# Triangular inverse in a cleared buffer of its own, basis norms taken from the inner products, and the rounding exponent by one integer operation

## The reference, cut to what matters

```python
G = Kc.T @ Kc + RIDGE_EPS * I            # 64 x 64
W = jnp.linalg.solve(G, Kc.T @ Vc)
U = I[:, :8]
for _ in range(2):
    U, _ = jnp.linalg.qr(W @ U)
S_new = 0.9 * S + U @ (U.T @ W)
out = 0.125 * (Qc @ S_new)
```

## Time and profile before

| | |
|---|---|
| runs, median (lowest to highest) | 1487.51 us (1479.54 to 1488.72) |
| profiled execution, its own time | 1489.35 us |
| its span, first to last instruction | 1487.5 us |
| TensorE matmul busy | 969.3 us (65%) |
| VectorE busy | 1230.2 us (83%) |
| ScalarE busy | 640.3 us (43%) |
| GpSimd busy | 231.3 us (16%) |
| TensorE's mean granted clock | 0.825 of full |

### The profile page before, as it was taken

How to read it: one execution, slowest core, us unless ns; L and a number is a source line. 1 busy time by engine, 2 the same in 40 slices (tenths; PEclk the granted TensorE clock), 3 DMA queues, 4 the chain that set the end, 5 groups by cost and what they waited for, 6 DMA issues and landing times.

```text
span 1487.5 us, 43627 instructions
## 1 busy us (share of the span) xinstructions
PE 969.3 (65%) x17726; PEld 780.0 (52%) x17726; DVE 1230.2 (83%) x3729; ACT 640.3 (43%) x1294; POOL 231.3 (16%) x149
## 2 busy tenths in 40 slices
PE   1443940389177799787799787852819825996175
PEld 0332530365167667677667686742717624775154
DVE  5885659949999779996799996798875798878997
ACT  3663630156135466555466454431416512563152
POOL 3552001101111001113102023012140000021000
PEclk9855985589579899899899898785959957898597
DMA  2555110001000001001101002030030200111000
GB/s 78 168 167 194 46 44 0 1 18 50 8 4 4 4 10 46 2 4 50 54 17 38 3 4 86 4 123 0 4 125 19 75 1 17 50 47 32 9 25 24
DMA packets 52086, 61.60 MB, mean 41 GB/s; under 512 B 4048, under 2 KB 32416, under 8 KB 51888
## 3 DMA queue, kind: packets, MB, share of 16 engines
q1 hardware_dynamic: 51888, 58.84, 12.6%
HBM read 38.31 MB, written 20.51 MB: 40 GB/s over the span
## 4 chain that ended last, share of the span: by engine, by line
DVE 36%; PE 32%; issue 13%; ACT 5%; POOL 2%; DMA 1%; SPq 0%; DVEq 0%; POOLq 0%; ACTq 0%
PE a_bank L840 5%; PE a_bank L830 3%; PE a_bank L846 3%; DVE a_total L1581 3%; DVE a_outer L1579 3%; DVE a_blocks L1584 3%; DVE a_outer L1575 2%; PE a_bank L946 2%; PE a_bank L961 2%; PE a_bank L769 2%; PE a_bank L898 2%; PE a_bank L698 2%; DVE a_blocks L1586 2%; DVE a_recip L1561 2%; PE a_bank L808 2%
## 5 line engine op out<-in xcount | busy, mean ns | idle before, releaser
L1092 ACT ACTIVATE a_work<-a_bank 128x512 f32<-128x512 f32 (+1 forms) x193 | 110.9, 599 | 206.5 <-PE a_bank L808 170.8
L1485 POOL TENSOR_TENSOR a_root<-a_recip,a_half 128x32 f32<-128x32 f32 (+2 forms) x24 | 89.8, 3743 | 655.8 <-DVEq L1570 636.9
L808 PE MATMUL a_bank<-a_ident,a_blocks 128*128 128x128 f32 x256 | 42.2, 340 | 162.6 <-DVE a_blocks L1595 162.6
L1092 ACT ACTIVATE a_solve<-a_bank 128x512 f32<-128x512 f32 (+2 forms) x184 | 87.9, 522 | 114.1 <-PE a_bank L846 53.9
L1575 DVE TENSOR_TENSOR a_outer<-a_blocks,a_weight 128x62 f32<-128x62 f32 (+15 forms) x248 | 129.4, 522 | 0.0
L1581 DVE TENSOR_REDUCE a_total<-a_outer 128x62 f32<-128x62 f32 (+30 forms) x248 | 127.0, 512 | 0.3
L808 PEld LDWEIGHTS a_bank<-a_ident,a_blocks 128*128 128x128 f32 x256 | 40.4, 208 | 163.7 <-DVE a_blocks L1595 163.7
L1579 DVE TENSOR_TENSOR a_outer<-a_blocks 128x60 f32<-128x60 f32 (+14 forms) x240 | 119.2, 497 | 0.7 <-DVE a_outer L1575 0.7
L1584 DVE TENSOR_TENSOR a_blocks<-a_blocks,a_outer 128x60 f32<-128x60 f32 (+14 forms) x240 | 118.3, 493 | 0.0
L698 PE MATMUL a_bank<-a_wk,a_cg 128*128 128x512 f32 x256 | 117.3, 602 | 0.0
L769 PE MATMUL a_bank<-a_scaled,a_blocks 128*128 128x352 f32 x256 | 90.6, 495 | 28.7 <-ACT a_scaled L1072 15.2
(11 more groups left out here) (200 smaller groups left out, 2402.4 us busy)
## 6 DMA issues: line engine op xcount, KB each, us to landing
f_x<-in_L_attn_x SPq DMA_DIRECT2D x16, 256.0 KB, 3.2
s_xnt<-f_xt SPq DMA_DIRECT2D x16, 256.0 KB, 2.1
s_c<-f_cm SPq DMA_DIRECT2D x16, 256.0 KB, 2.3
s_base<-f_base SPq DMA_DIRECT2D x16, 256.0 KB, 2.8
a_cg<-s_c SPq DMA_DIRECT2D x16, 256.0 KB, 2.9
a_cc<-s_c SPq DMA_DIRECT2D x16, 256.0 KB, 3.7
a_xnt<-s_xnt SPq DMA_DIRECT2D x16, 256.0 KB, 3.9
a_base_in<-s_base SPq DMA_DIRECT2D x13, 256.0 KB, 2.6
```

Of the source, the lines that this page charges most:

```text
L808: last = nc.tensor.transpose(bank[:, i * P:(i + 1) * P], rows_[:, :, 4 * rb + i], ident[:])
L1092: nc.scalar.activation(out, view, ACT.Copy, scale=scale).then_inc(emptied, 1)
L1485: nc.gpsimd.tensor_tensor(root[:, :, a:b], recip[:, :, a:b], half[:, :, a:b], ALU.pow).then_inc(roots_ok, 1)
```

## The change

`factor` gets a second buffer, `triangle`, of the same size. It is cleared and its diagonal set to one at the start of each call, before the wait for the call's input (which has moved into `factor`); `lead` and `schur` first wait for the end of the factor before, which used the buffer. The inverse grows in `triangle` (`x` in the code) and the factor stays in `block_` (`m`), so that the negated scaled columns stay there too. `weight` is gone: `known` multiplies by `m[:, :, 0:i, i]` in place. The update of the inverse covers one row more (`0:i` for `0:j`) and starts at step 0. The closing memsets are gone, and one multiplication over all 2 x 32 x 32 elements, from `x` to `m`, replaces two over parts.

`orthogonalise` multiplies a vector with itself and all later ones in one instruction; the first of the sums is the norm. The scaled copy is gone, and the sums are scaled instead. The two products L1626 are one instruction.

In `fp4_blocks` the exponent bits are ORed with a constant within L466; the clamp to 1.5 * 2**22 is the first half of two scalar_tensor_tensor instructions, which add it to, and subtract from it, the value. L467 is gone, and the sign that this turns is turned back in the last product.

The scratch for dynamic DMA descriptors is 4096 bytes where it was 8192.

```diff
--- before.py
+++ after.py
@@ -59,7 +59,7 @@
 T = GB_N * NC
 HB = 32
 KEPT = 16
-FACTOR_LINKS = 8 * (HB - 1) + 1
+FACTOR_LINKS = 7 * (HB - 1) + 4
 ROOTS = ((0, 16), (16, 28), (28, HB))
 LENGTHS = ((0, 6), (6, R))
 BANK = 512
@@ -444,7 +444,20 @@
...
+ROUNDER = 1.5 * 2.0 ** 22
+EXPONENT = 0x7F800000
+LARGE = (22 << 23) | (1 << 22)
...
 def fp4_blocks(nc, ch, jobs):
...
@@ -463,13 +476,12 @@
     each(lambda v, amax, scale, inv, step: V.tensor_scalar(scale, amax, 1.0 / 6.0, 1e-12, ALU.mult, ALU.max))
     each(lambda v, amax, scale, inv, step: V.reciprocal(inv, scale))
     each(lambda v, amax, scale, inv, step: V.tensor_tensor(v, v, bcast(inv, 2, QB), ALU.mult))
-    each(lambda v, amax, scale, inv, step: V.tensor_scalar(step.bitcast(I32), v.bitcast(I32), 0x7F800000, None, ALU.bitwise_and))
-    each(lambda v, amax, scale, inv, step: V.tensor_scalar(step, step, 1.0, 1.5 * 2.0 ** 22, ALU.max, ALU.mult))
-    each(lambda v, amax, scale, inv, step: V.tensor_tensor(v, v, step, ALU.add))
-    each(lambda v, amax, scale, inv, step: V.tensor_tensor(v, v, step, ALU.subtract))
+    each(lambda v, amax, scale, inv, step: V.tensor_scalar(step.bitcast(I32), v.bitcast(I32), EXPONENT, LARGE, ALU.bitwise_and, ALU.bitwise_or))
+    each(lambda v, amax, scale, inv, step: V.scalar_tensor_tensor(v, step, ROUNDER, v, ALU.max, ALU.add))
+    each(lambda v, amax, scale, inv, step: V.scalar_tensor_tensor(v, step, ROUNDER, v, ALU.max, ALU.subtract))
     for k, (v, amax, scale, inv, step, done) in enumerate(jobs):
         ch.wait(last[k])
-        V.tensor_tensor(v, v, bcast(scale, 2, QB), ALU.mult).then_inc(done, 1)
+        V.scalar_tensor_tensor(v, v, -1.0, bcast(scale, 2, QB), ALU.mult, ALU.mult).then_inc(done, 1)
...
 def fp4_weights(nc, ch, v, rows, nb, tmp):
@@ -572,7 +584,7 @@
         wkt, wvt, wqt = (blocks[:, i].rearrange("p (h m) -> p h m", m=P) for i in (1, 3, 5))
         recip, root, half = sb("recip", [P, 2, HB]), sb("root", [P, 2, HB]), sb("half", [P, 2, HB])
         outer_all = sb("outer", [P, 4 * KEPT * HB])
-        weight, total = sb("weight", [P, 2, HB]), sb("total", [P, 2, HB])
+        total, triangle = sb("total", [P, 2, HB]), sb("triangle", [P, 2, HB * HB])
         cg = [sb(f"cg{i}", [P, NC, D]) for i in range(2)]
         cc = sb("cc", [P, T, D])
         xa, xb, xc = (sb(n, [P, T, D]) for n in ("xa", "xb", "xc"))
@@ -1356,7 +1368,7 @@
         SUBSPACE_UNITS = 2 * (T // 4) + 2 * 2 + 2 * APPLY_UNITS + 4 + R // 4
         ASSEMBLE_UNITS = HB // 4 + 2 * (NQ // 32) + NQ // 8
 
-        LINKS = 2 * FACTOR_LINKS + 4 * R + 6 * (R - 1)
+        LINKS = 2 * FACTOR_LINKS + 4 * R + 3 * (R - 1)
 
         with nc.Block() as block:
 
@@ -1545,14 +1557,14 @@
                 dve.sem_inc(cg_used, 2)
                 dve.sem_inc(cc_used, 1)
 
-                def factor(block_, n, done):
...
-                    m = by_columns(block_)
-                    diagonal = block_[:, :, 0:HB * HB:HB + 1]
+                def factor(block_, n, given, done):
...
+                    m, x = by_columns(block_), by_columns(triangle[:])
+                    diagonal, ones = (y[:, :, 0:HB * HB:HB + 1] for y in (block_, triangle))
 
                     def area(at, a, b):
                         return outer_all[:, at:at + 2 * a * b].rearrange("p (s a b) -> p s a b", s=2, b=b)
@@ -1560,72 +1572,59 @@
                     def pivot(j):
                         return ch.inc(V.reciprocal(recip[:, :, j], m[:, :, j, j]))
 
+                    ch.link(V.memset(triangle[:], 0.0))
+                    ch.inc(V.memset(ones, 1.0))
+                    dve.wait_ge(*given)
                     ch.link(V.tensor_scalar(diagonal, diagonal, RIDGE_EPS, None, ALU.add))
                     inverse = pivot(0)
                     for j in range(HB - 1):
                         i, n_i = j + 1, HB - 1 - j
-                        row, rest = m[:, :, 0:j, j], m[:, :, 0:j, i:HB]
                         ch.wait(inverse)
                         if i in (ROOTS[0][1], ROOTS[1][1]):
                             dve.sem_inc(pivots_ok, 1)
-                        weights = ch.inc(V.scalar_tensor_tensor(weight[:, :, 0:i], m[:, :, i, 0:i], -1.0, recip[:, :, 0:i], ALU.mult, ALU.mult))
-                        column = ch.inc(V.scalar_tensor_tensor(m[:, :, j, i:HB], m[:, :, i:HB, j], -1.0, bcast(recip[:, :, j], 2, n_i), ALU.mult, ALU.mult))
-                        ch.wait(weights)
-                        terms = area(0, n_i, i)
-                        known = ch.inc(V.tensor_tensor(terms, m[:, :, i:HB, 0:i], bcast(weight[:, :, 0:i], 2, n_i), ALU.mult))
-                        if j:
-                            ch.wait(column)
-                            step = area(2 * KEPT * KEPT, j, n_i)
-                            product = ch.inc(V.tensor_tensor(step, bcast(m[:, :, j, i:HB], 2, j), bcast(row, 3, n_i), ALU.mult))
+                        ch.link(V.scalar_tensor_tensor(m[:, :, j, i:HB], m[:, :, i:HB, j], -1.0, bcast(recip[:, :, j], 2, n_i), ALU.mult, ALU.mult))
+                        terms, step = area(0, n_i, i), area(2 * KEPT * KEPT, i, n_i)
+                        known = ch.inc(V.tensor_tensor(terms, m[:, :, i:HB, 0:i], bcast(m[:, :, 0:i, i], 2, n_i), ALU.mult))
+                        product = ch.inc(V.tensor_tensor(step, bcast(m[:, :, j, i:HB], 2, i), bcast(x[:, :, 0:i, j], 3, n_i), ALU.mult))
                         ch.wait(known)
                         summed = ch.inc(V.tensor_reduce(total[:, :, 0:n_i], terms, op=ALU.add, axis=AX_X))
-                        if j:
-                            ch.wait(product)
-                            ch.inc(V.tensor_tensor(rest, rest, step, ALU.add))
+                        ch.wait(product)
+                        ch.inc(V.tensor_tensor(x[:, :, 0:i, i:HB], x[:, :, 0:i, i:HB], step, ALU.add))
                         ch.wait(summed)
                         ch.link(V.tensor_tensor(m[:, :, i:HB, i], m[:, :, i:HB, i], total[:, :, 0:n_i], ALU.add))
                         inverse = pivot(i)
                     ch.wait(inverse)
                     dve.sem_inc(pivots_ok, 1)
-                    for i in range(1, HB):
-                        V.memset(m[:, :, i, 0:i], 0.0)
-                    ch.link(V.memset(diagonal, 1.0))
                     dve.wait_ge(roots_ok, n * 3)
-                    V.tensor_tensor(m[:, :, 0:KEPT], m[:, :, 0:KEPT], bcast(root[:], 2, KEPT), ALU.mult)
-                    V.tensor_tensor(m[:, :, KEPT:HB, KEPT:HB], m[:, :, KEPT:HB, KEPT:HB], bcast(root[:, :, KEPT:HB], 2, KEPT), ALU.mult).then_inc(done, 1)
+                    V.tensor_tensor(m, x, bcast(root[:], 2, HB), ALU.mult).then_inc(done, 1)
 
                 def lead(g):
-                    dve.wait_ge(lead_in, g + 1)
-                    factor(lead_blocks, g * 2 + 1, lead_out)
+                    if not isinstance(g, int) or g:
+                        dve.wait_ge(schur_out, g)
+                    factor(lead_blocks, g * 2 + 1, (lead_in, g + 1), lead_out)
 
                 def schur(g):
-                    dve.wait_ge(schur_in, g + 1)
-                    factor(schur_blocks, g * 2 + 2, schur_out)
+                    dve.wait_ge(lead_out, g + 1)
+                    factor(schur_blocks, g * 2 + 2, (schur_in, g + 1), schur_out)
 
                 def orthogonalise(g):
 
                     dve.wait_ge(basis_in, g + 1)
                     for k in range(R):
-                        u = basis[:, k]
-                        sq = prod[:, 0:2 * DH].rearrange("p (s d) -> p s d", s=2)
-                        ch.link(V.tensor_tensor(sq, u, u, ALU.mult))
-                        ch.link(V.tensor_reduce(norm[:], sq, op=ALU.add, axis=AX_X))
-                        ch.link(V.tensor_scalar(norm[:], norm[:], 1e-30, None, ALU.max))
+                        n = R - k
+                        u, left = basis[:, k], basis[:, k:]
+                        pr = prod[:, 0:n * 2 * DH].rearrange("p (n s d) -> p n s d", s=2, d=DH)
+                        flat = lambda x: x.rearrange("p n s d -> p n (s d)")
+                        ch.link(V.tensor_tensor(flat(pr), flat(left), bcast(u.rearrange("p s d -> p (s d)"), 1, n), ALU.mult))
+                        ch.link(V.tensor_reduce(dots[:, 0:n], pr, op=ALU.add, axis=AX_X))
+                        ch.link(V.tensor_scalar(norm[:], dots[:, 0], 1e-30, None, ALU.max))
                         ch.link(V.reciprocal(dinv[:, :, k], norm[:]))
                         if k + 1 in (LENGTHS[0][1], LENGTHS[1][1]):
                             dve.sem_inc(norms_ok, 1)
-                        n = R - 1 - k
-                        if n:
-                            rest = basis[:, k + 1:]
-                            pr = prod[:, 0:n * 2 * DH].rearrange("p (n s d) -> p n s d", s=2, d=DH)
-                            ch.link(V.tensor_tensor(wvec[:], u, bcast(dinv[:, :, k], 2, DH), ALU.mult))
```

(13 more changed lines are left out.)

## The result

The changed kernel takes 1535.62 us in the median of 4 runs (1533.26 to 1538.05), the one before 1488.12 us (1479.54 to 1490.35, 4 runs). The ratio is 1.0331, with a 95% interval of 1.0293 to 1.0369. The forecast was 1519 us with a range of 1500 to 1558.

A forecast was written before the change was run, and what follows sets the result against it. Bound by a chain of waits, VectorE and TensorE in turn: factors +44, lead waits +5.6, orthogonalisation -3.9, roundings -8.7, -1.5 and -3.8 make +31.7 us on 1489.35, 1521; less 1.8 us to the median, 1519 us, range 1500 to 1558.

The forecast's parts named there:

- one index: `known` in the factor reads `m[:, :, 0:i, i]`, elements 128 bytes apart, costing 6.5 us a factor.
- Rival (a): The jump costs nothing in `known`'s long products of the five factors: 1481 us, not slower; chance 0.14.
- Rival (b): A long stream in `known` pays a whole element time, 1.05 ns, for each jump: 1558 us; chance 0.13.
- Rival (c): In the rounding, the OR costs L466 its rate, 1.05 ns an element: 1530 us; chance 0.03.
- The size of the jump: In `known`, 0.60 ns for each of 10,850 elements, from 0.55 to 0.67: 6.5 us a factor.
- The product and the update of the inverse: In the factor, the inverse's two instructions cover one row more, 1860 elements at 1.05 ns: 1.95 us a factor.
- The band that the prediction gave to its own mechanism: A jump of 0.5 to 0.8 ns in `known` gives 1511 to 1531 us; chance 0.60.
- The leads' room: Three hidden lead factors grow 10.8 us against room of 7.07, 10.07 and 9.59: TensorE waits 5.6 us more.
- rival d: TensorE's new waits before `lead_return` halve its clock, costing at most 2.5 us, inside the range; no separate chance given.
- What was forecast to be worth nothing: In the factor, removing `weight` was put at 0, removing the closing memsets at 0.1 us.
- The gains: Last orthogonalisation 3.9 us, ten late roundings 8.7, the one beside GpSimd's adds 1.5, three `hidden.vector` 3.8.
- the cover that I counted for the memsets: VectorE's idle time before Schur and first lead factors' input, 8.38 us and more, hides 2.0 us of clearing each.

The follow-up runs named there:

- step_1: Changed kernel, but `known` multiplies by a buffer of zeros read side by side (4 bytes apart), values not the reference's: 1483.35 us, ratio 0.9984 to the kernel before.
- weight_back: Changed kernel with the side-by-side buffer `weight` restored for `known`, all else kept: 1480.48 us, ratio 0.997 to the kernel before.
- step_32: Changed kernel, but `known` multiplies by zeros of the triangle lying 128 bytes apart, values not the reference's: 1536.89 us (one run).
- Step_2: Changed kernel, but `known` multiplies by zeros read 8 bytes apart, values not the reference's: 1476.04 us (one run).
- step_4: Changed kernel, but `known` multiplies by zeros read 16 bytes apart, values not the reference's: 1539.97 us (one run).
- gains_only: Kernel before with the new `fp4_blocks` and `orthogonalise` but the old factor: 1469.91 us, ratio 0.9864 to the kernel before.
- operands_swapped: Changed kernel with the two operands of `known` exchanged, the jumping one first: 1540.36 us (2 runs), ratio 1.039 to the kernel before.
- factor_only: Changed kernel with rounding and orthogonalisation as before, so the new factor alone: 1559.08 us, ratio 1.0483 to the kernel before.
- clear_twice: Changed kernel with the large memset that clears the triangle issued twice: 1544.44 us, ratio 1.0369 to the kernel before.
- step_3: Changed kernel, but `known` multiplies by zeros read 12 bytes apart, values not the reference's: 1496.92 us (one run).

## Why the prediction was right, step by step

**Direction and cause.** The forecast rested on one index, and the cause was that: step_1, weight_back and step_32 leave it no other. Rival (a), no cost in long products, falls: 1043 ns. Rival (b), a whole element time, falls too: the price is 0.70 ns ((1043 - 683) / 512, the 683 of the kernel before), not 1.05. The reading that decided was the growth of L1572 against L1571 in the earlier trace rows and the two forms of L1579 in the earlier trace rows, all of 60 elements or fewer; it carried over to 512 in kind, 15% low in size. The Trainium skill's note in "SBUF — State Buffer", Door 1: The DMA port swizzle, says that lines are 16 bytes and that at least two hits in each are needed for full rate. Step_2 (692 ns, free) and step_4 (1098 ns, full price) agree. Its other sentence, that fp32 can be strided for free by 4 elements, does not hold here if it is read as a step of 4: that step pays most of all. Rival (c), the OR at half the rate, falls by L479, 586 ns beside 587.

**The size of the jump** was the term too small. I took 0.60 ns, the trace has 0.69 to 0.82 in the groups from 224 elements on: `known` is busy 191.0 us in all where it was 129.4, 7.7 us a factor and not 6.5. The product and the update of the inverse took 2.5 us a factor more, not 1.95. So a Schur factor grew from 77.9 to 88.3 us in groups 1 and 2, and the five on the path by 50.4 us together (9.6, 10.1, 10.4, 10.4 and 9.8), where I had 44.

The band that the prediction gave to its own mechanism was too narrow at its upper end: for a jump of 0.5 to 0.8 ns it says 1511 to 1531 us, but from 0.6 to 0.8 the five factors add 10.9 us and the three leads, which it left out there, 6.5 more, so it should have ended at 1537. The measured jump lies inside that band of prices, and the measured 1535.6 us above that band of times.

**The leads' room.** Each new wait was longer than forecast: 7.8, 4.8 and 4.7 us for 3.7, 0.7 and 1.2. Two terms were mis-sized. From the Schur factor's end to their own the leads grew by 12.2, 11.4 and 11.4 us for the 10.8 of the forecast; the clearing in them took 2.4 us, not 2.0. And the room was smaller than the idle time of VectorE from which I read it: TensorE fetches the lead factor about 0.9 us before the basis reaches VectorE. Before, it began to at 488.47, 698.93 and 910.31 us (VectorE's basis products: 489.39, 699.85 and 911.22), 6.2, 9.2 and 8.7 us after the lead's end. From the Schur factor's closing product to TensorE's first transpose of the lead, the three stretches thus grew by 6.1, 2.3 and 2.8 us, 11.2 for the 5.6 of the sum. The rest of the waits was not a loss, since TensorE reached them 1.6 to 2.5 us earlier: in group 1 after 86.7 us where it took 89.2.

**The clock behind a new wait (rival d)** stays open. The stretch of group 0 from TensorE's first transpose of the lead to the next Schur factor (us, busy times by engine, granted clock), in the kernel before and in gains_only, both without a wait there:

```profile
488.50:531.90 43.40, 32.40 (x1129) 27.68 (x1128) 30.54 (x77) 20.52 (x42) 3.28 (x2) 0.88 0.02 4
```

```profile
486.00:530.20 44.20, 35.09 (x1128) 29.57 (x1127) 26.99 (x55) 20.52 (x42) 3.28 (x2) 0.81 0.02 4
```

In the changed kernel after its wait of 7.8 us, and in operands_swapped after one of 9.8 us:

```profile
510.90:557.90 47.00, 36.28 (x1127) 31.66 (x1128) 28.75 (x58) 20.12 (x40) 3.28 (x2) 0.81 0.02 4
```

```profile
515.80:560.30 44.50, 35.27 (x1127) 30.39 (x1128) 28.80 (x58) 20.23 (x40) 3.28 (x2) 0.83 0.02 4
```

The changed kernel took 3.6 us longer than the kernel before, at 0.81 for 0.88, above my bound of 2.5 us. But gains_only had the 0.81 without a wait, and operands_swapped with a longer wait took only 44.5 us. The other four kernels with a wait of over 7 us there (factor_only, clear_twice, step_4, step_32) took 46.9 to 48.3 us at 0.75 to 0.81, so a longer stretch mostly goes with the wait; that the wait makes it is not shown. The same stretches of groups 1 and 2 changed by -2.3 and +1.1 us (the latter at 0.79 for 0.76), and the one before the first Schur factor by -2.9, so over the kernel all four sum to -0.6 us.

**What was forecast to be worth nothing** was: the removed `weight` (weight_back beside step_1) and the removed memsets (0.08 us). Here the rows were read rightly; the closing memsets had the root's cover.

**The gains** summed to 16.5 us from the last factor's end to the end (60.5 us late there, 44.0 at the end), against 17.9: the orthogonalisation 4.0 for 3.9, a late rounding 0.86 for 0.87, the one beside GpSimd 0.87 for 1.5, since L480 took the whole slow slot. Sequence 12's rounding waited 1.4 us for ScalarE, which it did not before, nor in gains_only.

**The sum.** +50.4 + 11.2 - 0.6 - 16.5 is 44.5; the first factor began 0.45 us earlier, and the spans differ by 44.0. The forecast's +31.7 fell short by 6.4 in the factors, 5.6 at the leads and 1.4 in the gains; the other stretches gave 0.6 back. The medians differ by more than the traces, 47.5 us, since the profiled execution was the fastest of the changed kernel's four. The direction and the cause were read rightly. The size came out low, since the terms that were off erred the same way; the time lies inside the stated range without errors that cancel.

## What to carry to other kernels

An operand that jumps from line to line for every element made an fp32 two-operand pass of 512 elements 1.5 times as long (1043 for 683 ns), and the instruction that packed it was free where it could be issued beside another: price the address pattern of what stays before counting the instructions that go. Short strided instructions in a trace, of 60 elements and fewer, were enough to price long ones within 15% here; the growth with size, and two forms of one size that differ in the jump alone, gave the price, which the length of one instruction does not. Take the room of a waiting engine from the moment at which the consumer fetches, not from another engine's idle time. And separate the parts of a change: two of the three here were worth 1.4%, and one hid them; that one would have been a loss even without its jump.

## What the runs showed of the hardware that I had not expected

Jumps of 16 bytes and more are free while at most three addresses take turns (i = 1 to 3: 0.34 us for 174 elements beside 0.33), and cost 0.67 ns an element at four (0.15 us on 224). What counts looks to be lines of 16 bytes and not addresses. With four addresses 12 bytes apart, which lie in three such lines if the first lies at a line's start (bytes 0, 12, 24 and 36, an estimate, as the buffer's place was not looked up), step_3's `known` is free (0.39 us beside 0.39); with five, in four lines, it pays (0.54 beside 0.44), and so does step_4 with four addresses 16 bytes apart (0.54 beside 0.39). The rows of step_3 for both, then that of step_4:

```profile
209.27 0.39 DVE L1588 TENSOR_TENSOR a_outer<-a_blocks,a_zeros 128x224 f32<-128x224 f32 x1
...
211.24 0.54 DVE L1588 TENSOR_TENSOR a_outer<-a_blocks,a_zeros 128x270 f32<-128x270 f32 x1
```

```profile
209.20 0.54 DVE L1588 TENSOR_TENSOR a_outer<-a_blocks,a_zeros 128x224 f32<-128x224 f32 x1
```

Over 512 elements a distance of 12 bytes costs about half of what 16 bytes cost.

At the turn of VectorE's loop its first instruction started 4.72 and 4.51 us after the one before had ended, with nothing that it waited for in the profile (0.49 us of it lie before every large memset here):

```profile
545.69 1.76 DVE L1575 MEMSET a_triangle<- 128x2048 f32 x1 [4.72 <-issue]
...
778.24 1.76 DVE L1575 MEMSET a_triangle<- 128x2048 f32 x1 [4.51 <-issue]
780.11 0.19 DVE L1578 TENSOR_SCALAR a_blocks<-a_blocks 128x64 f32<-128x64 f32 x1
```

If the kernel before had this gap, it lay inside its wait for the Schur complement. So the cover that I counted for the memsets, 8.38 us, was not all free for them: in group 2 the memset ended at 780.00 us, and ScalarE's last write for the factor at 779.88. The same gap was 4.6 to 4.8 us in factor_only, step_32 and operands_swapped, and 2.1 to 2.4 us in weight_back, clear_twice and step_1 to step_4; what makes it was not tried.
